# A graph network on one core: the first mean stage makes h by nodes, with two PSUM banks for each product and an extra step of lag, and ScalarE begins the store

## What is computed

```python
def _L1_gnn_ref(fts, edge_index, W_l, W_r):
    ...
    seg_sum = jax.ops.segment_sum(fts[v], u, num_segments=n)
    aggregate = seg_sum / jnp.maximum(counts, 1.0)[:, None]
    out = fts @ W_l.T + aggregate @ W_r.T
    out = out / jnp.linalg.norm(out, axis=1, keepdims=True)
    return out
...
x = _layernorm(x + _L1_gnn_ref(x, ...), axis=-1)
...
h = x @ lin_w.T + lin_b      # the start of _L2_gnn_ref
```

## Time and profile before

| | |
|---|---|
| time, median of 3 runs | 5742.24 us (5740.17 to 5755.46) |
| the profiled execution's own time | 5690.39 us |
| its span, first to last instruction | 5688.5 us |
| DVE, ACT, PE, POOL busy over the span | 68%, 51%, 72%, 61% |
| granted TensorE clock, mean | 0.869 of full |
| the stage mean1 | 2402 to 3098 us, 696 us |

### The profile page before, as it was taken

One profiled execution on the slowest core, in us unless ns is written; L12 is line 12 of the kernel. 1 busy time (PEld: TensorE's weight loads), 2 busy tenths in 40 slices (PEclk: granted clock), 3 DMA queues, 4 the chain that ended last, 5 costly groups with the idle time before them and its releaser, 6 DMA issues. The chain is left out here.

```text
span 5688.5 us, 74909 instructions
## 1 busy us (share of the span) xinstructions
PE 4121.6 (72%) x16190; PEld 2482.6 (44%) x16190; DVE 3876.1 (68%) x13324; ACT 2879.9 (51%) x6489; POOL 3456.4 (61%) x3064
## 2 busy tenths in 40 slices
PE   4666759999994655566664779977897778956643
PEld 3333335555552333344443445544444344446643
DVE  5667769999995444377775786557665787746643
ACT  5444447777881000176664445534443565546644
POOL 5776668888876888645556660046203767755466
PEclk8888879999997777788887999989998899978876
DMA  2233334444433333556664775457545676757621
GB/s 46 75 84 86 76 93 140 140 140 141 141 121 79 62 62 62 76 183 196 196 197 152 196 210 146 128 174 214 169 142 155 195 201 200 205 184 231 200 83 60
DMA packets 778039, 802.10 MB, mean 141 GB/s; under 512 B 130880, under 2 KB 544776, under 8 KB 777466
## 3 DMA queue, kind: packets, MB, share of 16 engines
q1 hardware_dynamic: 436122, 420.60, 25.5%
q0 software_dynamic: 117504, 209.42, 15.3%
q10 hardware_dynamic: 223968, 167.29, 8.8%
HBM read 445.32 MB, written 351.66 MB: 140 GB/s over the span
## 5 line engine op out<-in xcount | busy, mean ns | idle before, releaser
L540 PE MATMUL gate_bank<-gate_ht,gate_whh 128*128 128x512 f32 x1764 | 869.3, 616 | 16.7 <-issue 7.5
L1023 POOL DMA_INDIRECT xh<-mean_xh,node_pos x392 | 377.8, 964 | 320.5 <-DVE mean_xh L1079 176.2
L540 PEld LDWEIGHTS gate_bank<-gate_ht,gate_whh 128*128 128x128 f32 x1764 | 338.5, 200 | 395.5 <-issue 372.0
L2275 PE MATMUL back_ps_sums<-back_same,back_rows 128*128 128x512 f32 x400 | 289.2, 890 | 285.8 <-DMA back_rows<-x_a,back_idx 285.8
L1665 POOL DMA_INDIRECT ffn_rows<-att_sums,up_idx x392 | 395.1, 1008 | 109.0 <-issue 108.2
L355 POOL DMA_INDIRECT gate_rows<-h_a,by_pos x200 | 195.8, 979 | 430.9 <-POOLq L118 326.5
L536 PE MATMUL gate_bank<-by_rank,gate_win 128*128 128x512 f32 x882 | 441.7, 601 | 6.2 <-ACT gate_z L671 5.9
L1702 PE MATMUL ffn_ps_u<-ffn_xs_t,up_up_w 128*128 128x512 f32 x784 | 387.0, 596 | 1.1 <-issue 1.1
L1709 PE MATMUL ffn_ps_f<-ffn_hg,up_f 128*128 128x512 f32 x784 | 386.5, 595 | 1.0 <-ACT ffn_hg L1867 1.0
L655 ACT ACTIVATE gate_r<-gate_bank,gate_b_rz 128x512 f32<-128x512 f32 x294 | 201.1, 684 | 328.5 <-PE gate_bank L540 165.6
L2256 POOL DMA_INDIRECT back<-back_out,back_dest x200 | 324.7, 1624 | 67.8 <-issue 60.1
(11 more groups left out here) (273 smaller groups left out, 11663.2 us busy)
## 6 DMA issues: line engine op xcount, KB each, us to landing
mean_x<-x_a SPq DMA_DIRECT2D x196, 256.0 KB
back<-blank SPq DMA_DIRECT2D x99, 264.0 KB
mean_rows<-back SPq DMA_DIRECT2D x98, 264.0 KB
hp<-mean_xh SPq DMA_DIRECT2D x98, 264.0 KB
gate_x<-xh SPq DMA_DIRECT2D x98, 264.0 KB
gate_hot<-hot_rows SPq DMA_DIRECT2D x100, 256.0 KB
ffn_x<-in_x_in SPq DMA_DIRECT2D x98, 256.0 KB
ffn_xr<-in_x_in SPq DMA_DIRECT2D x98, 256.0 KB
```

What stands on the lines that cost most here:

```text
L540: last = nc.tensor.matmul(bank_[:, :], whh[:, c * D:(c + 1) * D], ht[:, t.slot4, :], start=not inputs, stop=True)
L1023: nc.gpsimd.indirect_dma_start(out=g["xh"][:, :], out_offset=bass.IndirectOffsetOnAxis(ap=pos_all[:, t.n, j:j + 1], axis=0), in_=xh[:, t.n ...
L2275: last = nc.tensor.matmul(ps_sums[t.slot][:, :], rows[:, t.slot4, j, :], same[:, t.slot, j, :], start=j == 0, stop=j == J - 1)
```

## The change

1. h is made by nodes at once: four products of 128 columns with `yt` and `lin` give h with nodes on partitions, in `ps_h`. The product into `ps_ht`, the bias on ACT and the four turns back are gone. The bias is added by DVE as it takes h out of PSUM (a TENSOR_TENSOR add with `lin_b`, now on all partitions, in place of the COPY).
2. `ps_x`, `ps_y` and `ps_h` get two banks each, as `ps_v` had.
3. Lags grow so that nothing but the layer norm's short operations is handed over within a step: root 6, invert, shifts and apply 7, ps_y 8, yt 9, ps_h 10, h into xh 11, store and scatter 12. `res` and the layer norm's buffers get four slots.
4. DVE's step is put in another order. `statistics` is split into `row_statistics` (lag 5, last in the step), `aggregate` (lag 6) and `variance` (lag 6), and short operations stand between one that makes a value and one that reads it.
5. ACT begins the store to `hp`, at the end of its step with lag 12, in place of SP with lag 11. SP has only the two loads left.

The diff, cut:

```diff
+
+    def row_statistics(self, nc, dve, t, parts):
+
+        wait(dve, self.mv_done, t.n + 1 - self.slots)
+        for j, part in enumerate(parts):
+            last = nc.vector.bn_stats(self.stats[:, t.n % self.slots, j, :], part)
+        last.then_inc(self.stats_done, 1)
+
+    def aggregate(self, nc, dve, t):
+
+        wait_alone(dve, self.stats_done, t.n + 1)
+        wait(dve, self.shift_done, t.n + 1 - self.slots)
+        for j in range(J):
+            last = nc.vector.bn_aggr(self.mv[:, t.n % self.slots, j, :], self.stats[:, t.n % self.slots, j, :])
+        last.then_inc(self.mv_done, 1)
+
+    def variance(self, nc, dve, t):
+
+        wait(dve, self.mv_done, t.n + 1)
+        wait(dve, self.std_done, t.n + 1 - self.slots)
         nc.vector.tensor_scalar(self.var[:, t.n % self.slots, :], self.mv[:, t.n % self.slots, :, 1], EPS, None,
                                 ALU.add).then_inc(self.var_done, 1)
...
-        res = f.sb("res", [P, 2, J, D])
+        res = f.sb("res", [P, 4, J, D])
         xh = f.sb("xh", [P, STAGED, J, XH])
-        ln = LayerNormBuffers(f, "ln")
-        ps_x, ps_v = f.ps("ps_x"), [f.ps(f"ps_v{b}") for b in range(2)]
+        ln = LayerNormBuffers(f, "ln", 4)
+        ps_x, ps_v, ps_y, ps_h = ([f.ps(f"{n}{b}") for b in range(2)] for n in ("ps_x", "ps_v", "ps_y", "ps_h"))
...
-                if t := tile_at(11):
-                    wait(sp, id_done, t.n + 1)
-                    wait_alone(sp, h_done, t.n + 1)
-                    sp.dma_start(g["hp"][t.n * SUPER:(t.n + 1) * SUPER, :].rearrange("(p j) d -> p j d", j=J),
-                                 xh[:, t.n % STAGED, :, 0:WIDE]).then_inc(h_stored[t.n % STAGED], 16)
-            over_tiles(sp, NT, 11, step)
+            over_tiles(sp, NT, 0, step)
...
-                if t := tile_at(11):
+                if t := tile_at(12):
...
-            over_tiles(pool, NT, 11, step)
+            over_tiles(pool, NT, 12, step)
...
-                if t := tile_at(7):
+                if t := tile_at(8):
                     wait(pe, y_done, t.n + 1)
-                    wait(pe, yt_done, t.n)
-                    for j in range(J):
-                        last = nc.tensor.transpose(ps_y[:, j * P:(j + 1) * P], xh[:, t.n % STAGED, j, WIDE:XH],
+                    wait(pe, yt_done, t.n - 1)
+                    for j in range(J):
+                        last = nc.tensor.transpose(ps_y[t.slot][:, j * P:(j + 1) * P], xh[:, t.n % STAGED, j, WIDE:XH],
                                                    g["ident"][:, :])
                     last.then_inc(y_turned, 1)
...
-                    wait(pe, xt_done, t.n)
...
+                    wait(pe, xt_done, t.n - 1)
...
-                if t := tile_at(8):
+                if t := tile_at(10):
                     wait(pe, yt_done, t.n + 1)
-                    wait(pe, ht_done, t.n)
-                    nc.tensor.matmul(ps_ht[:, :], lin[:, :], yt[:, t.slot, :], start=True,
-                                     stop=True).then_inc(ht_made, 1)
-                if t := tile_at(9):
-                    wait(pe, ht_done, t.n + 1)
-                    wait(pe, h_done, t.n)
-                    for j in range(J):
-                        last = nc.tensor.transpose(ps_h[:, j * D:(j + 1) * D], ht[:, t.slot, j * P:(j + 1) * P],
-                                                   g["ident"][:, :])
-                    last.then_inc(h_turned, 1)
-            over_tiles(pe, NT, 9, step)
+                    wait(pe, h_done, t.n - 1)
+                    for j in range(J):
+                        last = nc.tensor.matmul(ps_h[t.slot][:, j * D:(j + 1) * D], yt[:, t.slot, j * P:(j + 1) * P],
+                                                lin[:, :], start=True, stop=True)
+                    last.then_inc(h_made, 1)
+            over_tiles(pe, NT, 10, step)
...
-                if t := tile_at(10):
-                    wait(dve, h_turned, t.n + 1)
-                    wait(dve, scattered[t.n % STAGED], 64 * (t.n // STAGED))
-                    wait(dve, h_stored[t.n % STAGED], 16 * (t.n // STAGED))
-                    nc.vector.tensor_copy(xh[:, t.n % STAGED, :, D:D + 3], tails[:, t.n, :, :]).then_inc(id_done, 1)
-                    nc.vector.tensor_copy(xh[:, t.n % STAGED, :, 0:D],
-                                          ps_h[:, :].rearrange("p (j d) -> p j d", j=J)).then_inc(h_done, 1)
+                if t := tile_at(5):
+                    wait(dve, length_done, t.n + 1)
+                    wait(dve, res_done, t.n - 1)
+                    nc.vector.reciprocal(inv_len[:, t.slot, :], length[:, t.slot, :]).then_inc(inv_len_done, 1)
...
+                if t := tile_at(6):
+                    ln.aggregate(nc, dve, t)
+                if t := tile_at(7):
+                    ln.invert(nc, dve, t)
+                if t := tile_at(11):
+                    wait(dve, scattered[t.n % STAGED], 64 * (t.n // STAGED))
+                    wait(dve, h_stored[t.n % STAGED], 16 * (t.n // STAGED))
+                    nc.vector.tensor_copy(xh[:, t.n % STAGED, :, D:D + 3], tails[:, t.n, :, :]).then_inc(id_done, 1)
+                if t := tile_at(6):
+                    ln.variance(nc, dve, t)
...
+                if t := tile_at(7):
+                    ln.shifts(nc, dve, t, y_done)
+                if t := tile_at(5):
+                    wait(dve, inv_len_done, t.n + 1)
+                    wait(dve, y_done, t.n - 3)
+                    wait(dve, ln.stats_done, t.n - 3)
+                    for j in range(J):
+                        last = nc.vector.scalar_tensor_tensor(
+                            res[:, t.slot4, j, :], v[:, t.slot4, j, :], inv_len[:, t.slot, j:j + 1],
+                            x[:, t.n % 8, j, :], ALU.mult, ALU.add)
+                    last.then_inc(res_done, 1)
...
-                if t := tile_at(6):
-                    ln.invert(nc, dve, t)
-                    ln.shifts(nc, dve, t, y_done)
...
-                    wait_alone(dve, inv_len_done, t.n + 1)
-                    wait(dve, y_done, t.n - 1)
-                    wait(dve, ln.stats_done, t.n - 1)
...
+                if t := tile_at(11):
+                    wait(dve, h_made, t.n + 1)
+                    nc.vector.tensor_tensor(xh[:, t.n % STAGED, :, 0:D],
+                                            ps_h[t.slot][:, :].rearrange("p (j d) -> p j d", j=J),
+                                            lin_b[:, :].unsqueeze(1).broadcast_to([P, J, D]), ALU.add).then_inc(h_done, 1)
                 if t := tile_at(5):
                     wait(dve, res_done, t.n + 1)
-                    ln.statistics(nc, dve, t, [res[:, t.slot, j, :] for j in range(J)], y_done)
-            over_tiles(dve, NT, 10, step)
+                    ln.row_statistics(nc, dve, t, [res[:, t.slot4, j, :] for j in range(J)])
+            over_tiles(dve, NT, 11, step)
...
-                    nc.scalar.activation(xt[:, t.slot, :], ps_x[:, :], ACT.Copy).then_inc(xt_done, 1)
+                    nc.scalar.activation(xt[:, t.slot, :], ps_x[t.slot][:, :], ACT.Copy).then_inc(xt_done, 1)
                 if t := tile_at(9):
-                    wait(act, ht_made, t.n + 1)
-                    wait(act, h_turned, t.n - 1)
-                    nc.scalar.activation(ht[:, t.slot, :], ps_ht[:, :], ACT.Identity,
-                                         bias=lin_b[:, :]).then_inc(ht_done, 1)
-                if t := tile_at(8):
                     wait(act, y_turned, t.n + 1)
-                    wait(act, ht_made, t.n - 1)
-                    nc.scalar.activation(yt[:, t.slot, :], ps_y[:, :], ACT.Copy).then_inc(yt_done, 1)
+                    wait(act, h_made, t.n - 1)
+                    nc.scalar.activation(yt[:, t.slot, :], ps_y[t.slot][:, :], ACT.Copy).then_inc(yt_done, 1)
...
-                if t := tile_at(6):
+                if t := tile_at(7):
                     wait(act, scattered[t.n % STAGED], 64 * (t.n // STAGED))
                     wait(act, y_turned, t.n + 1 - STAGED)
-                    ln.apply(nc, act, t, [res[:, t.slot, j, :] for j in range(J)],
+                    ln.apply(nc, act, t, [res[:, t.slot4, j, :] for j in range(J)],
                              [xh[:, t.n % STAGED, j, WIDE:XH] for j in range(J)], y_done)
-                if t := tile_at(5):
+                if t := tile_at(6):
                     ln.root(nc, act, t)
-            over_tiles(act, NT, 9, step)
+                if t := tile_at(12):
+                    wait(act, id_done, t.n + 1)
+                    wait_alone(act, h_done, t.n + 1)
+                    act.dma_start(g["hp"][t.n * SUPER:(t.n + 1) * SUPER, :].rearrange("(p j) d -> p j d", j=J),
+                                  xh[:, t.n % STAGED, :, 0:WIDE]).then_inc(h_stored[t.n % STAGED], 16)
+            over_tiles(act, NT, 12, step)
```

(24 more changed lines are left out.)

14 lines of the change are left out of this document (6 added, 8 removed).

## The result

The changed kernel takes 5694.1 us (median of 4 runs, 5682.7 to 5699.1), the kernel before beside it 5741.2 (4 runs): ratio 0.9905, 95% interval [0.9891, 0.9919]. By the medians it is 47 us faster, by the ratio some 55. Forecast were 116.

The account below looks back on a forecast made before the run. No engine is full; DVE's 5.51 us step plus 1.19 of stalls sets 6.70 us a tile. DVE's 4.95 + 0.3, plus 0.2 gives 5.45; 97 x (6.70 - 5.45) = 121, less 5: 5742 - 116 = 5626 us, range 5595 to 5712.

Parts of the forecast that it names:

- four places: DVE's waits ahead of statistics, aggregate, variance and tails' copy, 144.7 us in all; only aggregate's to stay, 0.3 us.
- lumps: DVE's stalls of 1 and 2 us that come with POOL's scatters, 1.19 us a step before the change.
- rival 1: The lumps persist at 1.19 us a step whatever the order, paid per scatter: 49 us faster, 5693; chance 0.33.
- forecast case of 5600 to 5650: The likeliest case, 5.3 to 5.7 us a tile, with 5626 us as its point; chance 0.47.
- 97 x (6.70 - 5.45): First mean stage's gain: 97 intervals, 6.70 us a tile falling to 5.45, 121 us, less 5 for added lag.
- POOL's 5.20 us a tile: Time POOL needs for a tile's four unchanged scatters when it waits for nothing, taken as a floor.
- PE's 24 passes: PE's passes of 128 columns after the change, some 5.1 us at the lower clock of 1.2 GHz.
- five long terms: In DVE's step: v, res, statistics, aggregates and the add of h, 3.81 us in sum.
- seven short operations: DVE's short operations in the new order, forecast at 0.6 to 1.5 us a step.
- SP's waits for h, 285.6 us: SP's waits ahead of the store, holding up only loads of x; they vanish, worth nothing.
- Rival 2: Something outside DVE sets 6.70 us a tile, so no change but the extra step: 5747 us; chance 0.12.
- Rival 3: Scatter traffic meets every DVE step, a 2.1 us lump in each, 7.05 us: 39 us slower, 5781; chance 0.08.

Follow-up runs that it names:

- a4_poolplain: Changed kernel with POOL issuing four plain DMAs per tile in node order in place of the four indirect ones: 5486.1 us, ratio to before 0.9548.
- a9_small: Changed kernel with plain row stores from SP, plus four indirect DMAs of 16 bytes a row per tile on POOL: 5677.8 us, ratio to before 0.9963.
- a10_small2: As a9_small, but two small indirect DMAs per tile instead of four: 5483.5 us, ratio to before 0.9615.
- a5: Changed kernel with four buffers of yt, so ACT's yt waits for an older product of h: 5707.1 us, ratio to before 0.9920.
- a8: Changed kernel with handovers spread over more steps and more buffers, run twice: 5675.3 and 5674.3 us, ratios to before 0.9958 and 0.9951.
- a13: Changed kernel with one pause on POOL behind the fourth scatter of a tile: 5698.9 us, ratio to before 0.9909.
- a14: Changed kernel with two pauses on POOL, behind the second and fourth scatter of a tile: 5705.7 us, ratio to before 0.9920.
- a11: Changed kernel with a small memset and a wait for it on POOL behind each indirect DMA: 5655.7 us, ratio to before 0.9913.
- a1_plain: Changed kernel with POOL's scatters replaced by four plain stores per tile from SP in node order: 5502.4 us, ratio to before 0.9568.
- c0_before: The kernel before, unchanged, run and profiled once more: 5749.7 us, ratio to before 1.0001, 6.94 us a tile.
- a7_sp13: Changed kernel with the store of h begun by SP at lag 13: 5699.7 us, ratio to before 1.0000.
- a2_spstore: Changed kernel with the store of h given back to SP at lag 12: 5743.0 us, ratio to before 0.9978.
- b4_gap2: Kernel before with two pauses on POOL, behind the second and fourth scatter of a tile: 5721.3 us, ratio to before 0.9937.

## Why the prediction was wrong

**The stalls: the step that failed.** I had "of the four places that one keeps its stall ... 0.3 us". DVE's stalls are 6.36 - 4.68 = 1.7 us a step, or 2.0 against the 4.39 of most steps without scatters. I had read the lumps as a property of a wait that comes straight after what it waits for, and removed most such waits. (The 144.7 us of idle at the four places could not all be stalls, which are 97 x 1.19 = 115 us; the rest are gaps that a step without a stall has too, and the steps outside the 97.) The runs showed that finished work is seen up to some microseconds late, by several engines, while POOL issues indirect DMAs back to back (a4_poolplain, a9_small and a10_small2 part the cases); new places only mean that another wait meets it.

5694 us lies within the stated range, which reached to 5712, only because the range took in rival 1; the forecast case of 5600 to 5650 did not come. In the sum 97 x (6.70 - 5.45) both terms were off: like against like it is 97 x (6.94 - 6.36) = 57 us (0.58 us a tile in place of 1.25), and the extra step of lag cost 1.7 us ahead of the first h (36.2 to 37.9 us from the stage's start), not 5.

**The floors.** POOL's 5.20 us a tile was taken as a floor that POOL could reach. It reaches it, and even 5.06, for two tiles and then stands. Seven kernels with four indirect DMAs a tile, the new order and the store on ScalarE lie at 6.2 to 6.4 us, whatever else was changed (after twice, a5, a8 twice, a9, a13, a14, and a11 by POOL's own pace). That, not DVE's work, is the pace of the stage now. PE's 24 passes are not: the clock is 0.76, forecast as lower than 0.83, but without the stalls (a1_plain) the same passes have 0.99 and fit into 4.4 us.

**DVE's step.** 4.95 forecast, 4.68 beside scatters, 4.38 without. The five long terms were right but for 0.05; the seven short operations, which I put at 0.6 to 1.5 us, took 0.9 beside scatters and 0.6 without.

**The store.** "SP's waits for h, 285.6 us, vanish, and are worth nothing" was the second wrong step, and the costliest for understanding: the move is worth 30 us on before, and in the changed kernel 42 (0.9978 - 0.9905 = 0.0073 of 5752) of the 55 that its ratio makes. I had looked only for someone who waits for SP's loads. The DMA view (2480 to 3020 us: packets, MB, share of the 16 engines) shows the store in SP's queue q1 in c0_before, and in a queue of its own, q10, after:

```profile
q1 hardware_dynamic: 62017, 61.03, 40.2%
...
q1 hardware_dynamic: 22430, 41.47, 26.9%
...
q10 hardware_dynamic: 44880, 22.98, 14.4%
```

The Trainium skill (DMA: Bandwidth & Descriptors, section Queues, rings and completion order) says the same: SP and ScalarE each have one ring of their own on each of the same DMA engines. Between 2500 and 2800 us of c0_before, q1 has packets under way for 56% of the time, and 55% of the time that the scatters' packets take falls where it has none; after the change these are 41% and 80%. That this is how the move helps is argued, not shown; a7_sp13, meant to part the queue from the wait, did not.

**The rivals.** Rival 1 named 5693 and the time is 5694, but that is luck: 4.95 + 1.19 = 6.14 us a tile was forecast and 4.68 + 1.68 = 6.36 measured, and before was at 6.94, not 6.70, by about as much. It was right that the price goes with the scatters, wrong that it is a constant beside DVE's work. Its own rule, lumps of 1.19 us kept, would have given a2_spstore 6.14 us a tile; it had 6.83. Rival 2 (a pace from outside DVE) comes nearer to the mechanism: in the new order there is such a pace, at 6.2 to 6.4 us with the store on ScalarE and 6.6 to 6.8 with it on SP (a7_sp13, a2_spstore). But it said "no change", and the store's move changed it. Rival 3, slower, did not come.

**Open.** What in the indirect DMAs makes other engines see finished work late (the list, the descriptors or the scattered writes); why two a tile don't and why a pause behind each, but not behind each second, lets POOL run through; how the store's place adds its 0.3 to 0.5 us a tile; what holds b4_gap2.

## What to carry to other kernels

A stall that ends at the same moment on several engines is not any engine's: ask what else ran then, before moving waits about. When a shorter step meets a stage that issues indirect DMAs nearly all the time, price the stage once with those DMAs replaced by plain ones; here those runs give 4.2 us a tile where the scatters leave 6.4, so the scatters, and not the order, were the larger term. And measure each part of a change by itself: the smallest edit, who begins a store, was most of this gain.

## What the runs showed of the hardware

Four indirect DMAs of 128 rows per tile (0.96 us each on POOL, 1.26 apart) raised a 4.39 us step of the other engines to 6.2 to 6.4 us, with rows of 1040 bytes or of 16; two per tile left most steps at 4.39. Plain DMAs from POOL (0.54 us each) cost the others nothing, at 4.23 us a tile and a DMA share of 0.97. SP, which otherwise began its load 0.08 us after the res it waited for, began it up to 4.5 us late in the changed kernel. The same kernel took 5700 us in some groups of runs and 5752 in others, and chip number 2 stands beside both.
